# Vision tower, token stage: raw patches turned, centred key/value weights, inverse deviations multiplied in behind the projection

## The reference, cut to what matters

```python
pe = conv(pixel_values, conv_w)                 # 81 patches of 256 channels for each image
grid = pe.reshape(b, C, h, CS, h, CS)
red = grid.mean(axis=(3, 5))                    # 9 windows: mean of their 9 patches
win = grid.transpose(...).reshape(b, hw, N, C)
q  = _ln(red, la_ln_q_g, la_ln_q_b) @ la_wq
kv = _ln(win, la_ln_kv_g, la_ln_kv_b) @ la_wkv  # keys and values of each patch
attn = softmax(einsum('bhnd,bhnkd->bhnk', q * scale, k_))
agg  = einsum('bhnk,bhnkd->bhnd', attn, v_)
local_out = red + agg @ la_proj_w + la_proj_b

def _ln(x, g, b):
    xc = x - mean(x)
    return xc * rsqrt(mean(xc * xc) + 1e-05) * g + b
```

## Time and profile before

| | |
|---|---|
| median of 3 runs (lowest to highest) | 796.1 us (794.16 to 797.16) |
| the profiled execution's own time | 795.92 us |
| its span, first to last instruction | 794.1 us |
| busy in the span | PE 710.0 us (89%), DVE 508.0, POOL 425.8, ACT 378.9 |
| mean granted clock of TensorE | 0.941 of full speed |

### The profile page before, as it was taken

The page is one execution under the profiler, slowest core; times in us unless marked ns, Lnnn a source line. Parts: engine busy times, 40 slices in busy tenths (PEclk is TensorE's granted clock), DMA queues, the critical chain, the costliest instruction groups (busy, mean ns, idle before and its releaser), DMA issues.

```text
span 794.1 us, 13086 instructions
## 1 busy us (share of the span) xinstructions
PE 710.0 (89%) x4247; PEld 607.2 (76%) x4247; DVE 508.0 (64%) x1228; ACT 378.9 (48%) x932; POOL 425.8 (54%) x360
## 2 busy tenths in 40 slices
PE   3999999999999999999828819999999999587898
PEld 3889998898989887554627718999999999344786
DVE  3688877877877777768989861332233223478957
ACT  4586665766666655433132413444444444066131
POOL 5777867768587761549769421433443332136640
PEclk9999999999999999999858958999999999689799
DMA  7955233332343030000020088999989881300001
GB/s 236 260 147 154 76 114 100 116 115 60 115 116 113 4 107 1 1 0 1 0 107 0 27 323 299 309 323 327 340 315 327 332 331 60 139 2 2 0 1 67
DMA packets 47084, 108.58 MB, mean 137 GB/s; under 512 B 5048, under 2 KB 24748, under 8 KB 39596
## 3 DMA queue, kind: packets, MB, share of 16 engines
q1 hardware_dynamic: 44428, 100.68, 37.9%
q0 software_dynamic: 2592, 7.10, 2.5%
HBM read 101.58 MB, written 6.17 MB: 136 GB/s over the span
## 4 chain that ended last, share of the span: by engine, by line
PE 76%; DVE 13%; DMA 3%; ACT 2%; POOL 2%; issue 2%; SPq 1%; DVEq 0%; ACTq 0%; POOLq 0%
PE banks L1728 12%; PE banks L1736 12%; PE banks L291 9%; PE banks L293 9%; PE banks L292 9%; PE banks L298 6%; PE banks L304 4%; PE banks L1336 3%; PE banks L1383 2%; DVE banks L1510 1%; PE banks L1310 1%; DVE a_o L1601 1%; DVE a_prod L1223 1%; PE banks L1366 1%; DMA xraw<-in_x_rest 1%
## 5 line engine op out<-in xcount | busy, mean ns | idle before, releaser
L417 POOL TENSOR_TENSOR x_lo<-xraw,x_hi 128x512 fp32r<-128x512 f32 x81 | 106.1, 1310 | 77.6 <-ACT x_hi L411 77.5
L1819 ACT ACTIVATE hid<-banks,b 128x128 f32<-128x128 f32 x216 | 79.3, 367 | 110.3 <-PE banks L1728 110.3
L291 PE MATMUL banks<-wc_hi,x_hi 128*128 128x256 f32 x324 | 97.9, 302 | 12.7 <-POOL x_hi L420 10.0
L293 PE MATMUL banks<-wc_hi,x_lo 128*128 128x256 f32 x324 | 93.0, 287 | 0.0
L292 PE MATMUL banks<-wc_lo,x_hi 128*128 128x256 f32 x324 | 92.8, 286 | 0.0
L1984 DVE TENSOR_TENSOR res<-banks,xb 128x256 f32<-128x256 f32 x27 | 11.5, 424 | 127.0 <-PE banks L1736 127.0
L1857 POOL TENSOR_TENSOR y<-bve,mhalf 128x1 f32<-128x1 f32 x27 | 20.4, 755 | 104.8 <-DVE bve L1992 104.8
L453 DVE BATCH_NORM_STATS2 stats<-banks 128x6 f32<-128x256 f32 x81 | 34.6, 427 | 62.8 <-ACT pe_sb L447 62.1
L291 PEld LDWEIGHTS banks<-wc_hi,x_hi 128*128 128x128 f32 x324 | 63.0, 194 | 14.8 <-issue 10.2
L1728 PEld LDWEIGHTS banks<-xT,w_raw 128*128 128x128 f32 x448 | 67.9, 196 | 5.8 <-ACT xT L1807 0.9
L291 PE MATMUL banks<-wkv_hi,xg_hi 128*128 128x512 f32 x162 | 70.4, 435 | 0.5 <-DVE prod L545 0.3
(11 more groups left out here) (334 smaller groups left out, 1856.2 us busy)
## 6 DMA issues: line engine op xcount, KB each, us to landing
w_raw<-in_w SPq DMA_DIRECT2D x28, 1024.0 KB, 6.7
xraw<-in_x_main SPq DMA_DIRECT2D x26, 768.0 KB
w1more<-in_w SPq DMA_DIRECT2D x13, 1024.0 KB, 5.9
w2more<-in_w SPq DMA_DIRECT2D x13, 1024.0 KB, 8.4
xraw<-in_x_rest SPq DMA_DIRECT2D x48, 96.0 KB
xraw<-in_x_rest SPq DMA_DIRECT2D x26, 114.0 KB
yl<-y_rows SPq DMA_DIRECT2D x2, 1028.0 KB, 6.9
a_w<-in_qkv_w SPq DMA_DIRECT2D x2, 768.0 KB, 5.3
```

The lines of the kernel that those rows point to most:

```text
L291: pe.matmul(dst, a[0], b[0], start=start, stop=False)
L293: return pe.matmul(dst, a[1], b[0], start=False, stop=stop)
L417: pool.tensor_tensor(x_lo[:, i % RING_X, :], xraw[:, k, 0:KF].rearrange("p c b -> p (c b)"), x_hi[:, i % RING_X, 0:KF * P], ALU.subtract). ...
L1819: act.activation(hid[:, s % 2, fc, :], bank(fc % 2, 0, P), ACT.Gelu, bias=b1[:, bass.ds(e * FC + fc, 1)]).then_inc(sem("gelu_made"), 1)
```

## The change

A layer norm before a linear map can be split: the centring goes into the weights once, and the inverse deviation can be multiplied in behind the product. So the patch itself is no longer normalized.

- ACT: `normalize_patch` is gone. `copy_v` becomes an Identity whose scale is the column of `rstd_w` of its patch.
- PE: `turn_patch` turns `pe_sb` as it is. Before the fourth convolution a second product with the key/value weights, of the gain divided by 256, gives the weights' weighted column mean.
- DVE: the weights are scaled and their mean is subtracted in one instruction with two tensor inputs and a scalar. `key_product` becomes a product of keys, `rstd_w` and query in one instruction. The early batch of variances and both shifts of patches are gone; the shift of the window's mean stays (`red_shift`).
- POOL: one power of 10 columns for each window (`window_std`, at the place of the late one) in place of two of 5 columns.
- The rings: `x_hi` and `x_lo` hold 7 patches in place of 8, `local` 4 windows in place of 9, `xg_hi` and `xg_lo` become one tile `xg`, and `localT` lies in `wkv_raw`.

```diff
-RING_X = 8
-RING_XN = 4
+RING_X = 7
+RING_LOCAL = 4
...
+        rstd_w = sb("rstd_w", [P, 2, T])
-        xg_hi = sb("xg_hi", [P, 2, C], F32R, tok)
-        xg_lo = sb("xg_lo", [P, 2, C], F32R, tok)
+        xg = sb("xg", [P, 2, 2, C], F32R, tok)
...
-        xn = wkv_raw[:, :, :].rearrange("p c (t n) -> p (c t) n", n=C)
-        local = sb("local", [P, NW * C], F32, tok)
+        local = sb("local", [P, RING_LOCAL * C], F32, tok)
...
-        tail_hi, tail_lo = xg_lo[:, 0, :], xg_lo[:, 1, :]
...
+        tail_hi, tail_lo = xg[:, 1, 0, :], xg[:, 1, 1, :]
...
-        CLASS_ROW = 2
-        def window_batch(n, late):
-            return 2 * n + late + (n > 0)
+        CLASS_ROW = 1
+        def window_batch(n):
+            return n + (n > 0)
...
         def copy_pe(act, i):
             if i >= RING_PE:
-                act.wait_ge(sem("xn_made"), i - RING_PE + 1)
+                act.wait_ge(sem("xT_done"), i - RING_PE + 1)
             act.wait_ge(sem("conv_done"), i + 1)
             act.activation(pe_sb[:, i % RING_PE, :], bank(i % 2), ACT.Copy).then_inc(sem("pe_copied"), 1)
...
-        def early_variances(dve, n):
...
-            dve.tensor_scalar(veps[0][:, 0:EARLY_KEYS], mv[0][:, 0:EARLY_KEYS, 1], 1e-5, None, ALU.add).then_inc(sem("var_made"), 1)
-        def late_variances(dve, n):
+        def window_variances(dve, n):
...
-            dve.tensor_scalar(veps[0][:, EARLY_KEYS:NP], mv[0][:, EARLY_KEYS:NP, 1], 1e-5, None, ALU.add)
+            dve.tensor_scalar(veps[0][:, 0:NP], mv[0][:, 0:NP, 1], 1e-5, None, ALU.add)
...
             dve.tensor_scalar(veps[0][:, NP:T], mv[0][:, NP:T, 1], 1e-5 * NP * NP, None, ALU.add).then_inc(sem("var_made"), 1)
-        def early_std(pool, n):
...
-                pool.wait_ge(sem("xn_made"), NP * (n - 1) + EARLY_KEYS)
-            inverse_std(pool, window_batch(n, 0), 0, EARLY_KEYS)
-        def late_std(pool, n):
...
                 pool.wait_ge(sem("redn_made"), n)
-            inverse_std(pool, window_batch(n, 1), EARLY_KEYS, T)
...
-        def patch_rows(j):
...
-        def normalize_patch(act, j):
...
-            normalize(act, patch_rows(j), pe_sb[:, j % RING_PE, :], k).then_inc(sem("xn_made"), 1)
+            if n > 1:
+                pool.wait_ge(sem("key_used"), NP * (n - 1))
+            pool.wait_ge(sem("var_made"), window_batch(n) + 1)
+            pool.tensor_tensor(rstd_w[:, n % 2, :], veps[0][:, :], mhalf[:, :], ALU.pow).then_inc(sem("rstd_made"), 1)
+        def red_shift(dve, n):
+            dve.wait_ge(sem("rstd_made"), window_batch(n) + 1)
+            dve.scalar_tensor_tensor(out=nmr[0][:, NP:T], in0=mv[0][:, NP:T, 0], scalar=-1.0, in1=rstd_w[:, n % 2, NP:T],
+                                     op0=ALU.mult, op1=ALU.mult).then_inc(sem("nmr_made"), 1)
...
         def turn_patch(pe, j):
-            pe.wait_ge(sem("xn_made"), j + 1)
+            pe.wait_ge(sem("pe_copied"), j + 1)
             if j >= 2:
-                pe.wait_ge(sem("xg_lo_made"), j - 1)
-            turn(pe, bank(2 + j % 2), patch_rows(j)).then_inc(sem("xT_done"), 1)
-        def split_xT_hi(act, j):
...
+        def copy_xg(act, j):
...
-            act.activation(xg_hi[:, j % 2, :], bank(2 + j % 2), ACT.Copy).then_inc(sem("xg_hi_made"), 1)
-        def split_xT_lo(dve, j):
+            act.activation(xg[:, j % 2, 0, :], bank(2 + j % 2), ACT.Copy).then_inc(sem("xg_hi_made"), 1)
+        def split_xg(dve, j):
...
-            dve.tensor_tensor(xg_lo[:, j % 2, :], bank(2 + j % 2), xg_hi[:, j % 2, :], ALU.subtract)\
-               .then_inc(sem("xg_lo_made"), 1)
+            dve.tensor_tensor(xg[:, j % 2, 1, :], bank(2 + j % 2), xg[:, j % 2, 0, :], ALU.subtract).then_inc(sem("xg_made"), 1)
...
+            if k == 0:
+                act.wait_ge(sem("rstd_made"), window_batch(n) + 1)
             act.wait_ge(sem("kv_done"), j + 1)
-            act.activation(v_sb[:, n % 2, k, :], bank(4 + j % 2, C, 2 * C), ACT.Copy).then_inc(sem("kv_copied"), 1)
+            act.activation(v_sb[:, n % 2, k, :], bank(4 + j % 2, C, 2 * C), ACT.Identity, scale=rstd_w[:, n % 2, k:k + 1])\
+               .then_inc(sem("kv_copied"), 1)
...
             dve.wait_ge(sem("kv_copied"), j + 1)
-            dve.tensor_tensor(prod[:, k * C:(k + 1) * C], bank(4 + j % 2), q_sb[:, :], ALU.mult).then_inc(sem("key_used"), 1)
+            dve.scalar_tensor_tensor(out=prod[:, k * C:(k + 1) * C], in0=bank(4 + j % 2), scalar=rstd_w[:, n % 2, k:k + 1],
+                                     in1=q_sb[:, :], op0=ALU.mult, op1=ALU.mult).then_inc(sem("key_used"), 1)
...
-            normalize(act, redn[:, :], red_sum[:, n % 2, :], NP).then_inc(sem("redn_made"), 1)
+            act.activation(redn[:, :], red_sum[:, n % 2, :], ACT.Identity, scale=rstd_w[:, n % 2, NP:T], bias=nmr[0][:, NP:T])\
+               .then_inc(sem("redn_made"), 1)
...
+                    copy_xg(act, j + 1)
...
-                if j + 2 < NJ:
-                    normalize_patch(act, j + 2)
...
-                if k == 4:
-                    early_std(pool, n + 1)
                 if k == NP - 1:
-                    late_std(pool, n + 1)
+                    window_std(pool, n + 1)
...
-                    early_variances(dve, n + 1)
...
-                if k == 5:
-                    shift_of(dve, window_batch(n + 1, 0), 0, EARLY_KEYS)
...
                 if k == 7:
-                    late_variances(dve, n + 1)
+                    window_variances(dve, n + 1)
                 if k == 8:
-                    shift_of(dve, window_batch(n + 1, 1), EARLY_KEYS, T)
+                    red_shift(dve, n + 1)
...
-                    pe.wait_ge(sem("wkv_prepared"), CH)
-                    mm_rows(pe, bank(4, 0, 2 * C), aggT, wkv_raw, 0, 2 * C).then_inc(sem("kvb_done"), 1)
+                    pe.wait_ge(sem("wkv_prepared"), 2 * CH)
+                    mm_rows(pe, bank(4, 0, 2 * C), aggT, wkv_raw, 0, 2 * C)
+                    mm_rows(pe, bank(5, 0, 2 * C), agg, wkv_raw, 0, 2 * C).then_inc(sem("kvb_done"), 1)
...
                         act.activation(aggT[:, c * P:(c + 1) * P], vecs[:, LAKV + 2 + c:LAKV + 3 + c].broadcast_to([P, P]), ACT.Copy)\
                            .then_inc(sem("wkv_prepared"), 1)
+                        act.activation(agg[:, c * P:(c + 1) * P], vecs[:, LAKV + c:LAKV + 1 + c].broadcast_to([P, P]), ACT.Copy,
+                                       scale=1.0 / C).then_inc(sem("wkv_prepared"), 1)
...
                         act.activation(wkv_hi[:, c, :], wkv_raw[:, c, :], ACT.Copy).then_inc(sem("wkv_copied"), 1)
...
                 if i == LEAD:
-                    normalize_patch(act, 0)
                     copy_pe(act, NP - 1)
...
-                dve.tensor_scalar(wkv_raw[:, c, :], wkv_raw[:, c, :], vecs[:, LAKV + c:LAKV + c + 1], None, ALU.mult)\
-                   .then_inc(sem("wkv_prepared"), 1)
-            for i in range(2, EARLY_KEYS):
+                dve.scalar_tensor_tensor(out=wkv_raw[:, c, :], in0=wkv_raw[:, c, :], scalar=vecs[:, LAKV + c:LAKV + c + 1],
+                                         in1=bank(5, 0, 2 * C), op0=ALU.mult, op1=ALU.subtract).then_inc(sem("wkv_prepared"), 1)
...
-            early_variances(dve, 0)
...
-            shift_of(dve, 0, 0, EARLY_KEYS)
-            for i in range(EARLY_KEYS + 1, NP):
+            for i in range(5, NP):
                 measure(dve, i)
-            late_variances(dve, 0)
```

More of the change, by code:

```diff
@@ L399, in vision_tower @@
         BEHIND = 4
-        EARLY_KEYS = 5
         def split_x_hi(act, i):
@@ L695, in turn_local @@
             pe.wait_ge(sem("redT_made"), CH * min(n + 3, NW))
-            turn(pe, bank(6), local[:, n * C:(n + 1) * C]).then_inc(sem("local_turned"), 1)
+            turn(pe, bank(6), local_at(n)).then_inc(sem("local_turned"), 1)
         def copy_localT(act, n):
@@ L1717, in turn_rows @@
                     pe.wait_ge(sem("tables_made"), 2)
-                turn(pe, bank(6 + s % 2), xg[:, s % AHEAD, :]).then_inc(sem("rows_turned"), 1)
+                turn(pe, bank(6 + s % 2), xrows[:, s % AHEAD, :]).then_inc(sem("rows_turned"), 1)
             def up(s, fc):
```

67 lines of the change are left out of this document (29 added, 38 removed).

## The result

| | kernel before | changed kernel |
|---|---|---|
| median of 15 runs (lowest to highest) | 794.33 us (792.89 to 797.16) | 798.22 us (796.67 to 799.57) |
| ratio, 95% interval | | 1.0040 (1.0031 to 1.0050) |
| span of the profiled execution | 794.1 us | 797.8 us |

A forecast was written before the change was run, and what follows sets the result against it. PE was taken as the bound, busy without a gap from 60 to 300 us, leaving only head and tail: 1.87 + 0.42 + 0.16 + 0 + 1.31 = 3.76 us on 795.92 or 796.1, predicted 799.8, range 797.2 to 802.2.

The forecast's parts named there:

- The full stretch: From 60 to 300 us PE is busy for all 240 us, so work taken from ACT, DVE or POOL shortens nothing.
- the middle: Windows inside PE's 240 us: longer power still covered, DVE has time free, smaller pixel ring adds no wait; 0 us.
- The head, weights: Before the fifth convolution: four more PE passes, 1.60 us, and two longer DVE weight instructions, 0.27; together 1.87 us.
- my second rival: In the windows, POOL holds DVE's new key products up; 808 us at 1 us for each of 8 windows; chance 0.08.
- The head, first power: Ahead of the first window: the 10-column power delays `nmr` and the `wkv_lo` products that PE awaits; 0.42 us.
- The head, first window: In the first window: longer copy of values, 0.10, and longer key product, 0.06, reach PE; 0.16 us.
- The tail: From 307.3 to 331 us: power 0.76, key products 0.13 and 0.26, last copy and product 0.16; together 1.31 us.
- ACT's relief in the tail: Rival, token stage's end: patches no longer queue behind ACT's 0.6 us normalization; 798.2 us, chance 0.22.
- Another clock in later stages: Rival, untouched stages after the token stage: they start later and are granted another clock; 791 us, chance 0.04.
- The sum: Whole kernel: terms of head, middle and tail add to 3.76 us, 0.47% more than the median of 796.1 us.
- The signs named for the tail: In the changed profile: the piece at 315.21 about 3.3 us later, the one at 327.69 about 3.6 later.

The follow-up runs named there:

- e4: Changed kernel with ACT's normalization of each patch put back, 79 of them, into a scratch tile nobody reads; 799.17 us, ratio 1.0058 to the kernel before.
- r1: The changed kernel measured and traced once more, nothing edited; 798.37 us, ratio 1.0043 to the kernel before.
- e1: Changed kernel without the second product of the key/value weights, which are multiplied by the scales only; 796.19 us, ratio 1.0015 to the kernel before.
- b3: Kernel before with one unused tile of 32 bytes per partition among the small tiles, no instruction changed; 795.50 us, ratio 0.9998.
- b2: Kernel before with one unused tile of 80 bytes per partition among the small tiles, no instruction changed; 795.65 us in one run.
- e5: Changed kernel with the second product of the weights moved behind the fourth convolution; 795.99 us, ratio 1.0012 to the kernel before.
- e7: Changed kernel with the second product behind the fourth convolution and the mean's column first in the power; 794.67 us, ratio 1.0001 to the kernel before.
- e8: Changed kernel with second product behind fourth convolution, mean's column first, and low half of weights made between measurements of patches 6 to 8; 795.27 us, ratio 1.0001.
- e2: Changed kernel with each window's power in two parts again, five columns early and five late; 796.17 us, ratio 1.0013 to the kernel before.
- e6: Changed kernel with the power split, the mean's one column first, then the patches' nine; 795.70 us, ratio 0.9998 to the kernel before.
- e3: Changed kernel with values copied without a scale and key products from two tensors, inverse deviation left out; 797.21 us, ratio 1.0029 to the kernel before.

## Why the prediction was right, point by point

**The full stretch: right.** "PE's 240 us are the cover": 240.00 of 240 still, and e4 shows that ACT's 47.6 us, put back, cost a full window nothing. Predicted for the middle was 0, measured -0.50. The term is off by an effect that the prediction did not have: the same instructions lasted less long with their tiles at other places.

**The head, weights: 1.87 predicted, 2.0 measured at the same place of the dip.** The term was right and a little small. The second product cost more than its 1.60: its first pass starts 1.71 us behind the first pass of the first product in r1, where no dip lies over them. The 1.60 were read from four passes of which the first 0.57 us lay in a dip, up to the start of the next convolution. The longer writes cost 0.24 between the first two traces and 0.19 by e1, 0.27 predicted. DVE's two new instructions end 1.40 to 1.41 us after they begin in each of the ten traces that have them; the old ones take 1.16, 1.22 and 1.21 (before, b3, e1) and, in b2, 2.31:

```profile
22.16 0.69 DVE L2325 COPY kvb<-banks 128x512 f32<-128x512 f32 x1 [2.87 <-PE banks L299]
22.77 2.31 DVE L2327 TENSOR_SCALAR wkv_raw<-wkv_raw,vecs 128x512 f32<-128x512 f32 x2
...
22.89 0.67 POOL L421 TENSOR_TENSOR x_hi<-xraw,x_hi 76x128 fp32r<-76x128 f32 x1
23.53 1.26 POOL L418 TENSOR_TENSOR x_lo<-xraw,x_hi 128x512 fp32r<-128x512 f32 x1
24.77 0.63 POOL L421 TENSOR_TENSOR x_hi<-xraw,x_hi 76x128 fp32r<-76x128 f32 x1
```

There the head has no dip, so they begin at 22.77 instead of 23.87 and meet POOL while it works without a pause. They are 1.1 us longer, and POOL's own short instructions take 0.67 and 0.63 instead of 0.45. The same shows, smaller, in the kernel before, e1 and b3, where one of POOL's short instructions takes 0.64 beside the old form. Beside the new form it takes 0.45 to 0.46, in the five traces (r1, e4, e5, e7, e8) in which they meet; in the other five POOL pauses then. In all four traces of the old form the second instruction ends 0.28 to 0.29 us after one of POOL's: after `x_lo` in b2 (24.79), after the short one in the others.

That DVE waits here for POOL's instruction to end is seen better where DVE's part is tiny. In the kernel before, the five variances of a window take 0.17 us with POOL at rest (29.14). In the eight later windows they start amid an instruction of POOL, take 0.69 to 1.13 us, and end within 0.04 us of its end, as here:

```profile
29.14 0.17 DVE L466 TENSOR_SCALAR veps<-mv 128x5 f32<-128x5 f32 x1
...
188.62 2.40 POOL L638 TENSOR_TENSOR vprod<-vprod 128x1024 f32<-128x1024 f32 x1
190.14 0.91 DVE L466 TENSOR_SCALAR veps<-mv 128x5 f32<-128x5 f32 x1
190.99 1.29 POOL L417 TENSOR_TENSOR x_lo<-xraw,x_hi 128x512 fp32r<-128x512 f32 x1
```

Not every such instruction is held: 0.15 us sufficed for a variance at 107.75 (`L970`), while POOL was in an instruction. So the old form, a product within SBUF, can be held up by POOL, and the new one, with a bank as an input, was not in the five traces where they met. It is the reverse of my second rival. Without a dip the changed kernel's head takes 18.22 (r1) against 17.42 (b2), only 0.8 more; with b2's 1.1 us of hold-up taken off, 1.9 more, near the predicted size. How often the kernel before is held up like this is not known: b2 is the one trace of it without a dip in the head. The Trainium skill, "SBUF — State Buffer", section "SBUF: two separate sides", has a lock for which VectorE in one of its 2-port modes and GpSimd take turns, each for a whole instruction; by that rule the old form could wait and the new one not, and these rows agree.

**The head, first power: 0.42 predicted, 0.53 measured.** The power takes 1964 ns (1943 predicted) and e2 and e6, with the shorter late power, each take the whole 0.53 away.

**The head, first window: +0.16 predicted, -0.05 measured.** The term was too small and an offset was missing. The operands cost 0.30 in windows 0 and 1 (e3) and the single power another 0.27 (e2), while at most 0.17 of ACT's relief (e4 against the changed kernel) and an estimated 0.07 from the placement stand against it. The rest of the offset was not found. This stretch is also too unsteady for so small a sum: b2 takes 0.36 longer there than the kernel before, with the same instructions. That the term came within 0.2 is not to its credit.

**The tail: 1.31 predicted, 1.36 measured.** Its parts hold as well: the power 0.76 predicted, 0.71 by e2; the operands 0.55 predicted, 0.60 by e3. They hold along the chain too: from the power to the piece that was at 315.21 it is 8.24 us instead of 7.31, 0.93 more (0.76 + 0.13 predicted), from there to the last piece 0.26 more (0.26), and from there to the last turn 0.15 more (0.16).

**The rivals.** ACT's relief in the tail fell by e4 (0.03 us) and by the 0.05 that e2 and e3 leave. POOL does not hold the key products up: 475 ns in the mean of 81 and none above 485, 479 predicted, with POOL busy for 169 of 240 us. The same section of the Trainium skill left open whether a scale column counts as an SBUF input; by these 475 ns it does not here. Another clock in later stages: the dip at 332 to 336 us does come and go, and between two traces of the same kernel the stretch behind the last turn is 0.90 longer with it, but it is the execution's and not the change's.

**The sum.** 3.76 predicted, 3.7 between the profiled spans, 3.2 (2.5 to 4.0) by the ratio. That the spans agree so well is chance. What the table gives the change itself is 2.00 + 0.53 - 0.05 - 0.50 + 1.36 = 3.3 us, near the ratio; the place of the dip in the head and the stretch behind the last turn, where nothing was changed, add 0.2 and 0.3. Within the 3.3 the errors cancel in part: the weights, the first power and the tail are 0.29 above their terms, the first window and the middle 0.71 below. The signs named for the tail came sooner than forecast for the same reason: the piece that was at 315.21 came 3.03 later instead of 3.3, the copy at 327.69 came 3.29 later instead of 3.6. With r1's trace as the changed kernel's, the difference of the spans would have been 1.4. The time itself came 1.6 under the forecast, and that is its base: 796 there, 794.3 in the median of 15. The prediction took 0.5% for the least that a measurement can tell from no change; with 15 runs on each side the interval is 0.1% to either side, so a slowdown of 0.4% is clear of none.

## What to carry to other kernels

Work taken off an engine while TensorE is busy without a gap pays nothing here; what the change costs at the two ends, where nothing covers it, is the whole price. Look at which column of a batched operation the chain waits for and make that one alone and first (549 ns instead of 1964): with the product's move that brought the changed kernel back to the time of the kernel before, though not below it. Before trusting a difference of 1 or 2 us between two traces, take a second trace of one of the kernels and compare stretches between the same instructions, with the same clock in them.

## What the runs showed of the hardware

- One stretch of 3.4 us at the granted clock 0.5 near 18 us of the head, 6.8 us in one trace, came in ten of 14 traces and was missing in four; the one at 332 to 336 us came in seven and was missing in seven. No edit was needed for either. The later the head's dip began, the longer the head: from 7.62 to 9.17 us behind the first convolution, 19.59 to 19.98 us.
- A window of TensorE that waits for nothing took 34.09 us in the kernel before, 34.07 with an unused tile of 32 bytes among the small tiles and 34.00 with one of 80 bytes, with the same instructions; each value repeated to 0.01 in all five full windows. The changed kernel and its variants took 33.99. What it is in the placement stays open.
- DVE's product of a tile with a scalar column, SBUF to SBUF with 512 columns, took 1198 ns in the mean where it met POOL's uninterrupted work (b2), and 617 in the kernel before. DVE's addition on 5 columns within SBUF took 172 ns beside a resting POOL and 694 to 1131 when it started amid an instruction of POOL, ending with it.
- The power on POOL takes 0.55 us for one column and some 0.157 for each further one (549 ns for 1, 1806 for 9, 1964 for 10).
